# Fetching the selected rows of an attention mask by an indirect DMA instead of a product with a one-hot matrix

## The reference, cut to what matters

```
x = layernorm(x + attention(x))                      # 16 heads of 8, tanh soft cap, causal
weights = x @ router_w + router_b                    # one number a token
sel_idx = sort(top_k(weights, 64)[:63])              # the chosen tokens of a batch
x_sel, pos_sel, w_sel = x[sel_idx], position_ids[sel_idx], weights[sel_idx]
m_sel = attention_mask[b, 0][sel_idx][:, sel_idx]    # 63 x 63 values of a 512 x 512 mask
sc = q @ k.T / sqrt(8) + m_sel                       # rotary attention among the chosen tokens
out = x; out[sel_idx] = processed(x_sel) * w_sel     # plus x for the tokens not above the threshold
x = layernorm(x + out)
```

## Time and profile before

| | us |
|---|---|
| median of 3 runs | 994.78 |
| lowest, highest | 991.25, 1000.37 |
| span of the profiled execution | 992.9 |
| mean granted TensorE clock in it | 0.792 of 2.4 GHz |

### The profile page before, as it was taken

One profiled execution on the slowest core, in us unless ns is written; L12 is line 12 of the kernel. 1 busy time (PEld: TensorE's weight loads), 2 busy tenths in 40 slices (PEclk: granted clock), 3 DMA queues, 4 the chain that ended last, 5 costly groups with the idle time before them and its releaser, 6 DMA issues.

```text
span 992.9 us, 17000 instructions
## 1 busy us (share of the span) xinstructions
PE 777.2 (78%) x5488; PEld 443.0 (45%) x5488; DVE 710.4 (72%) x2141; ACT 610.8 (62%) x403; POOL 412.1 (42%) x776
## 2 busy tenths in 40 slices
PE   3389887989688978898698869898689969764653
PEld 2244343544455444544464445545454445343432
DVE  4632648668868887877887787977887886767444
ACT  0198778668766786677485866677576958800000
POOL 4144425444436444542544443642545344501100
PEclk9997667879788997897697877897697969965555
DMA  5010000002000102000100002000100000000001
GB/s 169 0 33 1 12 12 21 2 2 106 22 1 2 44 1 65 1 1 0 39 25 0 1 0 64 0 1 0 53 0 0 2 20 24 1 1 22 0 1 43
DMA packets 30340, 19.65 MB, mean 20 GB/s; under 512 B 1459, under 2 KB 27587, under 8 KB 30275
## 3 DMA queue, kind: packets, MB, share of 16 engines
q1 hardware_dynamic: 30274, 18.89, 6.3%
HBM read 14.69 MB, written 4.19 MB: 19 GB/s over the span
## 4 chain that ended last, share of the span: by engine, by line
PE 51%; DVE 31%; issue 12%; ACT 3%; POOL 1%; DVEq 1%; POOLq 0%; ACTq 0%
PE ps_s L1123 10%; PE ps_y L1137 9%; PE ps_m L1238 4%; PE ps_a L1187 4%; PE ps_m L1144 3%; DVE junk L893 3%; PE ps_m L1205 3%; PE ps_a L1175 2%; PE ps_a L1168 2%; PE ps_m L1298 2%; PE ps_m L1337 2%; PE ps_m L1284 2%; PE ps_m L1223 2%; ACT pr L664 2%; PE ps_m L1321 1%
## 5 line engine op out<-in xcount | busy, mean ns | idle before, releaser
L652 ACT ACTIVATE th<-ps_s 128x1024 f32<-128x1024 f32 (+1 forms) x256 | 310.1, 1236 | 192.0 <-PE ps_s L1123 186.8
L664 ACT ACTIVATE pr<-th 128x2560 f32<-128x2560 f32 x128 | 298.6, 2334 | 32.8 <-PE ps_y L1137 32.8
L1123 PE MATMUL ps_s<-q_st,k_st 32*128 32x512 f16 (+3 forms) x1024 | 207.9, 338 | 10.1 <-ACT th L652 6.9
L560 POOL TENSOR_SCALAR_AFFINE_SELECT pr<-pr 128x256 f32<-128x256 f32 (+2 forms) x512 | 198.8, 421 | 0.0
L1137 PE MATMUL ps_y<-pr,v_aug 128*32 128x512 f32 (+3 forms) x2048 | 172.1, 482 | 3.4 <-POOL pr L560 3.4
L1123 PEld LDWEIGHTS ps_s<-q_st,k_st 32*128 32x128 f16 x1024 | 83.4, 101 | 101.0 <-issue 55.8
L617 POOL TENSOR_TENSOR pool_mark<-head_of 128x1 f32<-128x1 f32 x128 | 27.3, 213 | 216.0 <-ACT pr L664 215.9
L574 POOL TENSOR_TENSOR st<-qk,st 128x1024 f16<-128x1024 f32 x32 | 73.0, 2301 | 101.7 <-DVE st L800 101.7
L1137 PEld LDWEIGHTS ps_y<-pr,v_aug 128*32 128x32 f32 x2048 | 63.7, 119 | 108.9 <-issue 91.7
L1187 PE MATMUL ps_a<-ident,st 128*128 128x128 f16 x512 | 57.4, 281 | 39.6 <-POOL st L574 23.6
L1187 PEld LDWEIGHTS ps_a<-ident,st 128*128 128x128 f16 x512 | 44.5, 127 | 62.3 <-issue 42.8
(11 more groups left out here) (186 smaller groups left out, 1258.6 us busy)
## 6 DMA issues: line engine op xcount, KB each, us to landing
masks<-in_L_ffn_attention_mask SPq DMA_DIRECT2D x5, 1024.0 KB, 5.9
x_in<-in_L_attn_x SPq DMA_DIRECT2D x16, 256.0 KB, 3.2
x_res<-in_L_attn_x SPq DMA_DIRECT2D x16, 256.0 KB, 3.2
result<-y_out SPq DMA_DIRECT2D x16, 256.0 KB, 2.4
w_sb<-in_L_ffn_w SPq DMA_DIRECT2D x2, 256.0 KB
pr<-in_L_attn_w_q SPq DMA_DIRECT2D x1, 64.0 KB, 1.9
pr<-in_L_attn_w_k SPq DMA_DIRECT2D x1, 64.0 KB, 2.0
pr<-in_L_attn_w_v SPq DMA_DIRECT2D x1, 64.0 KB, 2.0
```

The lines of the kernel that those rows point to most:

```text
L560: return nc.gpsimd.affine_select(out=buf, in_=buf, compare_op=ALU.is_ge, fill=0.0, base=0, pattern=[[0, n], [1, P]] if n > 1 else [[1, P]] ...
L652: nc.scalar.activation(th[:, gi % 2, c0:c1], ps_s[:, c0:c1], ACT.Tanh, scale=1.0 / (QK_SCALE ** 2 * DH ** 0.5 * SOFTCAP))\
L664: nc.scalar.activation(pr[:, gi % 4, :], th[:, gi % 2, :], ACT.Exp, scale=SOFTCAP)\
L1123: last = mm(ps_s[:, c:c + S - P * kb], k_st[32 * j:32 * j + 32, k, g, P * kb:P * kb + P], q_st[32 * j:32 * j + 32, k, g, P * kb:S], start= ...
```

## The change

The chosen rows no longer come by a product. The table `trig` gets a 17th column with the number of the token's row among the 4 x 512 mask rows, so the gathering product brings that number along in `xs`. A new step `sel.row` on POOL, last in the slot of `sel.zb`, waits for `xs`, converts the number to an integer and issues one indirect DMA that reads 128 rows of 2 KB from the mask in HBM into `R`, now a buffer of its own. Step `sel.RT` waits for that DMA. The steps `sel.R` of PE and DVE, the five loads of mask tiles, and the wait of `route.w` for the buffer that `R` shared are gone. POOL's iterations are all written out now instead of looping. In the setup, POOL has one iota, one conversion and a longer first wait more, and DVE and PE wait for 18 instead of 16 setup steps.

```diff
-    [], ["prep.st0/0@1", "sel.R@-1", "prep.st1/0@1"],          # PE_ORDER
+    [], ["prep.st0/0@1", "prep.st1/0@1"],
...
-    ["fin.root1/0@0 & late.root1@-2", "sel.R@-1", "fin.root2/0@0 & late.root2@-2"],     # VE_ORDER
+    ["fin.root1/0@0 & late.root1@-2", "fin.root2/0@0 & late.root2@-2"],
...
-    [], ["prep.sq/0@1", "sel.zb@-1"],                          # POOL_ORDER
+    [], ["prep.sq/0@1", "sel.zb@-1", "sel.row@-1"],
...
-    "sel.R": ["sel.vv1@0"],                                    # BANK_READ
-    "sel.qkT": ["sel.R@0"],
+    "sel.qkT": ["sel.vv1@0"],
...
-        masks = sb("masks", [P, 2, NT, S])
-        trig = sb("trig", [P, NPC, 2 * DH])
+        trig = sb("trig", [P, NPC, 2 * DH + 1])
+        row_i = sb("row_i", [P, NPC], I32)
+        mask_row = sb("mask_row", [P, 1], I32)
...
-        xs = sb("xs", [P, D + 1 + 2 * DH])
+        xs = sb("xs", [P, D + 2 + 2 * DH])
...
-        R = w_wide
+        R = sb("R", [P, S])
...
+            nc.gpsimd.iota(row_i[:, :], pattern=[[P, NPC]], base=0, channel_multiplier=1).then_inc(const_ready, 1)
+            pool.wait_ge(const_ready, 8)
...
+            nc.gpsimd.tensor_copy(trig[:, :, 2 * DH], row_i[:, :]).then_inc(const_ready, 1)
+            pool.wait_ge(const_ready, 15)
...
+            def sel_row(q, _):
+
+                ve["sel"].wait(pool, q, "xs")
+                if q > 0:
+                    pool.wait_ge(mask_fetched, q * 16)
+                pl["sel"].done(nc.gpsimd.tensor_copy(mask_row[:, :], xs[:, D + 1 + 2 * DH:]), "row", q)
+                pl["sel"].wait(pool, q, "row")
+                pe["sel"].wait(pool, q - 1, "RT")
+                nc.gpsimd.indirect_dma_start(
+                    R[:, :], None, amask.rearrange("m o s j -> (m o s) j"),
+                    bass.IndirectOffsetOnAxis(ap=mask_row[:, 0:1], axis=0), bounds_check=MASKS * S - 1,
+                    oob_is_err=False).then_inc(mask_fetched, 16)
...
-            iterations(pool, body, 3, PAIRS - 2)
+            for p in range(-1, PAIRS + 3):
+                body(p)
...
-                if k == 0:
-                    pe["sel"].wait(v, b.pair - 1, "RT")
...
-                ve["sel"].wait(t_, q, "R")
+                t_.wait_ge(mask_fetched, q * 16 + 16)
                 bank_free("sel.RT", q)
```

More of the change, by code:

```diff
@@ L67 @@
     "sel": ["xs", "ss"] + newton("r1", 1) + newton("r1", 2) +
-        ["hn", "ET", "hnT", "cosp", "sin0", "sin1", "rope", "vv0", "vv1", "R", "qkT", "RT", "msel"],
+        ["hn", "ET", "hnT", "cosp", "sin0", "sin1", "rope", "vv0", "vv1", "qkT", "RT", "msel"],
     "att": ["sc0", "mx0", "sub0", "sc1", "mx1", "sub1", "den", "rden", "PT0", "PT1", "o0", "o1", "oT", "x1f",
@@ L77 @@
     "route": ["wrow"],
-    "sel": ["gather", "ET", "hnT", "qkv", "R", "qkT", "RT", "msel"],
+    "sel": ["gather", "ET", "hnT", "qkv", "qkT", "RT", "msel"],
     "att": ["S0", "S1", "P0T", "P1T", "PV", "oT", "wo", "h2T", "w1"],
@@ L84 @@
     "route": ["xw"],
-    "sel": ["zb0", "zb1"],
+    "sel": ["zb0", "zb1", "row"],
     "att": ["kw0", "kw1", "hh", "hu"],
@@ L400, in build @@
         zeroed = sem("zeroed")
-        mask_loaded = sem("mask_loaded")
+        mask_fetched = sem("mask_fetched")
         x_in_loaded = [sem(f"x_in_loaded{i}") for i in range(2)]
@@ L461, in _ @@
         def _(sp):
-            def load_mask(m, k):
-                sp.dma_start(masks[:, k], amask[m, 0].rearrange("(c p) j -> p c j", p=P)).then_inc(mask_loaded, 16)
             for i, (w, t) in enumerate(((w_q, 0), (w_k, 1), (w_v, 2), (w_o, 3))):
@@ L478, in _ @@
             sp.dma_start(pos_i[:, :], pos.rearrange("b (c p) -> (b c) p", p=P)).then_inc(weights_in, 16)
-            for k in range(2):
-                load_mask(k, k)
             def load_res(b, k):
@@ L505, in body @@
                     load_x(Batch(p, 4), 0)
[L507 to L511, removed]
                 if live(p - 2, PAIRS):
@@ L528, in _ @@
             nc.gpsimd.iota(slot_i[:, :], pattern=[[1, SLOTS]], base=0, channel_multiplier=0).then_inc(const_ready, 1)
-            pool.wait_ge(const_ready, 7)
+            nc.gpsimd.iota(row_i[:, :], pattern=[[P, NPC]], base=0, channel_multiplier=1).then_inc(const_ready, 1)
+            pool.wait_ge(const_ready, 8)
             nc.gpsimd.affine_select(out=ident[:, :], in_=ident[:, :], compare_op=ALU.not_equal, fill=1.0, base=0,
@@ L540, in _ @@
             nc.gpsimd.tensor_copy(slot_no[:, :], slot_i[:, :]).then_inc(const_ready, 1)
-            pool.wait_ge(const_ready, 13)
+            nc.gpsimd.tensor_copy(trig[:, :, 2 * DH], row_i[:, :]).then_inc(const_ready, 1)
+            pool.wait_ge(const_ready, 15)
             nc.gpsimd.affine_select(out=head_of[:, :], in_=head_of[:, :], compare_op=ALU.is_ge, fill=0.0, base=DH - 1,
@@ L605, in att_hu @@
                 pl["att"].done(mul(hu[:, :], hq[:, :], hb[:, :]), "hu", q)
-            table = {"prep.sq": prep_sq, "prep.lo": prep_lo, "route.xw": route_xw, "sel.zb": sel_zb, "att.kw": att_kw,
+            table = {"prep.sq": prep_sq, "prep.lo": prep_lo, "route.xw": route_xw, "sel.zb": sel_zb, "sel.row": sel_row, "att.kw": att_kw,
                      "att.hh": att_hh, "att.hu": att_hu}
@@ L680, in _ @@
             v.wait_ge(attn_weights_in, 16 * 4)
-            v.wait_ge(const_ready, 16)
+            v.wait_ge(const_ready, 18)
             for half in range(2):
@@ L929, in sel_gather @@
                 ve["late"].wait(v, q - 1, "proc")
-                ve["sel"].done(nc.vector.tensor_copy(xs[:, :], ps_m[:, 0:D + 1 + 2 * DH]), "xs", q)
+                ve["sel"].done(nc.vector.tensor_copy(xs[:, :], ps_m[:, 0:D + 2 + 2 * DH]), "xs", q)
             sel_ET = copy_step("sel", "ET", lambda: nc.vector.tensor_copy(ET[:, :], ps_m[:, :]),
                                [(pe["late"], lambda q: q - 1, "sc1")])
-            sel_R = copy_step("sel", "R", lambda: nc.vector.tensor_copy(R[:, :], ps_m[:, :]),
-                              [(ve["route"], lambda q: Batch(q, 1), f"eq{NT - 1}")])
             def sel_squares(q, _):
@@ L1077, in _ @@
                      "route.row": route_row, "route.ge": route_ge, "route.eq": route_eq, "route.rank": route_rank,
-                     "sel.xs": sel_gather, "sel.ET": sel_ET, "sel.R": sel_R, "sel.ss": sel_squares, "sel.hn": sel_hn,
+                     "sel.xs": sel_gather, "sel.ET": sel_ET, "sel.ss": sel_squares, "sel.hn": sel_hn,
                      "sel.RT": sel_RT, "sel.hnT": sel_hnT, "sel.qkv": sel_qkv, "sel.msel": sel_msel,
@@ L1098, in _ @@
             tr = nc.tensor.transpose
-            t_.wait_ge(const_ready, 16)
+            t_.wait_ge(const_ready, 18)
             t_.wait_ge(attn_weights_in, 16 * 4)
@@ L1224, in sel_gather @@
                     for c in range(NT):
-                        last = mm(ps_m[rows, D + 1:D + 1 + 2 * DH], E[:, c, rows],
+                        last = mm(ps_m[rows, D + 1:D + 2 + 2 * DH], E[:, c, rows],
                                   trig[:, NT * trig_row(Batch(q, k)) + c, :], start=(c == 0), stop=(c == NT - 1))
@@ L1345, in _ @@
                      "fin.yT": fin_yT, "fin.wo": fin_wo, "route.wrow": route_wrow, "sel.gather": sel_gather,
-                     "sel.ET": sel_ET, "sel.R": sel_R, "sel.RT": sel_RT, "sel.hnT": sel_hnT, "sel.qkv": sel_qkv,
+                     "sel.ET": sel_ET, "sel.RT": sel_RT, "sel.hnT": sel_hnT, "sel.qkv": sel_qkv,
                      "sel.msel": sel_msel, "sel.qkT": sel_qkT, "att.S0": lambda q, _: att_scores(q, 0),
```

## The result

The changed kernel takes **1026.3 us** (median of four runs, 1024.4 to 1026.9) against 996.6 before (991.3 to 1000.4, four runs on the same chip): ratio 1.028, 95% interval 1.024 to 1.033. It is 2.8% slower where 993 was forecast, and lies outside the range. The profiled execution has a span of 1025.2 us, 32.3 more than before.

A forecast was written before the change was run, and what follows sets the result against it. PE and DVE hand work to each other, neither alone setting the pace. Gain 11.2 us (6.3 in pairs 0 to 5, 4.9 in 6 and 7) against 11.1 of cost: no change, forecast 993 us, range 981 to 1009.

The forecast's parts named there:

- the wait at `pv.0`: Second batch's `pv.0` on PE waits for POOL's masking, 2.4 us late; 1.0 us passes on in pair 4, 9.1 in all.
- the clock there: The wait at `pv.0` may let the clock fall one step earlier; 1.5 us in all.
- the price of a `pv` block at the lower clock: A `pv` step takes 3.91 us at 1.2 GHz and 2.36 at 2.4, a factor of 1.65; used behind the removed product.
- 24.4 minus 13.2: Removing the product gains 24.4 us through PE; the low clock behind its place takes back 13.2 in six pairs.
- The reading of the cover: Three of the product block's 5.6 us in pair 4 are hidden behind DVE; the next step starts 2.6 us earlier.
- the upper bound of that term, 22: Clock cost in six pairs if the whole stretch behind the removed product runs at 1.2 GHz; 13.2 was taken.
- The last pair: No other work fills the product's block there, so DVE's path gives 3.8 us of gain.
- pair 6: No transposes stand behind the product's block there, so DVE is the later one; 1.1 us of gain.
- The DMA: The fetched rows land before `sel.RT`, in pair 4 25 us behind the issue, so nothing of the transfer shows.
- The loads, the 17th column and the written-out loop: Removing five mask loads, widening the gather product and copy, and writing out POOL's loop: 0 each.
- the three things that I said would show me wrong: Issue under 0.6 or over 2 us on POOL, clock 1.00 behind the transposes, or PE waiting for the DMA.
- The long issue on POOL: Rival, chance 0.18: the DMA issue behind `xs` is long, 7 us per us; 1009 us at 3.5 us of issue.

The follow-up runs named there:

- e1: The changed kernel with `sel.row` moved six slots later on POOL, behind the two masking groups `pv.0` waits for; 994.0 us, ratio to before 0.997.
- e2: The kernel before with `sel.row` added into a spare buffer, product kept, POOL's loop written out, one set of mask tiles; 1029.0 us, ratio 1.029.
- e6: The changed kernel with eight unused products added on PE ahead of `pv.0`, where PE waits; 1010.5 us, ratio to before 1.014.
- e5: The changed kernel without the indirect DMA, POOL's wait and conversion kept, mask left out of the result; 1008.4 us, ratio to before 1.008.
- e10: The changed kernel with `sel.row` six slots later on POOL and three unused products where the mask product stood; 986.3 us, ratio to before 0.987.
- e4: The kernel before with POOL's loop written out and nothing else; 994.8 us, ratio 0.999.
- e3: The changed kernel without `sel.row`, `R` a constant zero and the mask left out; 991.3 us, ratio to before 0.994.

## Why the prediction was wrong

**The step that failed: the wait at `pv.0`**, the term that priced the issue on POOL with "two groups ... 2.4 us late, and `pv.0` of PE with them" and "1.0 us passes on", 9.1 us in all, and the clock there at "1.5 us in all". The mechanism is the one named (e1, e2); the size is 31 us instead of 10.6. Two things were mis-sized. POOL was later than worked out: 3.5 us, since between the conversion and the DMA that reads its result POOL stands idle 0.79 us, which I had not counted, and the masking groups took 0.36 more behind it (3.60 us for 3.24). The wait for `xs`, 1.11 against 0.95, the conversion, 0.30 against 0.25, and the issue, 1.06 against 1.2, were right. With 1.4 of slack 2.1 us pass on instead of 1.0, and in the whole kernel 16 us. The larger error is the clock: I put it at 1.5 us in all, and it takes 15 us (e6), 1.3 to 2.1 us at each `pv.0`. A right size of the wait would not have saved the sum: in e5 waits of 1.24 to 1.56 us brought the low clock too, in six of seven pairs. The prediction used the price of a `pv` block at the lower clock only at the other end of the pair, and misread the row: 3.91 us is a block in which the clock rose. A window over it, and a `pv` block of the same trace that is at 1.2 GHz throughout:

```profile
603.58:607.49 3.91, 3.91 (x34) 1.31 (x34) 2.89 (x6) 0.00 (x0) 1.04 (x1) 0.59 0.91 259
...
120.60 4.50 PE L1137 MATMUL ps_y<-pr,v_aug 128*32 128x512 f32 x32
```

So the factor is 4.50 / 2.36 = 1.91 and not 1.65.

**The product was worth even less than 24.4 minus 13.2.** The reading of the cover was right: without the product the step behind it starts 0.06 us after DVE's copy, PE idles 2.3 us ahead of it, the clock stands at 0.50, as forecast, and in e1 it comes 2.5 us sooner behind `xs` (19.9 us against 22.4), where 2.6 was worked out. Over six pairs it starts 17.0 us sooner (19.2 by the rows; the prediction's 19.5 is a slip of 0.3). But the clock took all of it, not half: `pv.1` needs 4.29 to 4.50 us, not 3 to 3.9, which is 12.3 us in six pairs, the transposes ahead of it take 5 us more, and the second column of the table is 52.9 us in e1, 52.8 before. These 17 us lie nearer the upper bound of that term, 22, than its 13.2, which rested on the assumption that the clock would rise as long after the start of the block as it had after that of the product; in e1 it hardly rose within `pv.1` in any of the six pairs. e10 shows the other side: with the clock up the same removal is worth 12.7 us at this place.

**The last pair** gave 3.5 us in e1, for 3.8, and **pair 6** nothing, for 1.1. **The DMA** landed 3.4 us after its issue and no instruction of PE waited for it, as said. **The loads, the 17th column and the written-out loop** show no cost (e4 for the last; e3, which has all three changes, is faster than the kernel before). Of the three things that I said would show me wrong none came: the issue takes 1.06 us, the clock behind the transposes is low, nothing waits for the DMA. They watched the terms I was unsure of, and the failure came from one that I had thought small.

**The rivals.** The long issue on POOL had the right place and direction and the wrong price: at 1.06 us it was not long, and its rule, 7 us for each us of lateness, held only until the clock fell with it. (By that rule and 993 the kernel is level with the one before at an issue of 1.5 us and 1% slower at 2.9, not at 1.9 and 2.6.) The Trainium skill (page "SBUF — State Buffer", section "SBUF: two separate sides") has such a DMA wait for its descriptors while VectorE holds the shared port; the issue here took 1.06 us in the changed kernel and 1.63 at the late place (medians), beside a busy VectorE both times, so the 1.9 us more of issue in the estimate of about 1006 were not there. The rows landed 3.4 and 4.0 us after the issue; no run has this DMA beside an idle VectorE, so whether any of that was such a wait is not shown.

Of a clock that falls in every round the Trainium skill tells too (page "TensorE: Matmul & The Clock Gate", section "HAM oscillation — how this bites in real kernels"): a kernel whose TensorE waits in each tile pays the low clock in each tile anew. This case agrees, with 15 us in seven pairs for waits of 3.2 to 3.8 us.

**What stays open.** Why one of four waits of 1.56 us left the clock up in e5, no run settles, nor why the issue takes 0.6 us longer at the late place. Nor is it shown why the stretch from `RT` to the next `xs` is 3 to 6 us longer than before in the three other kernels of the table.

## What to carry to other kernels

Where a step is added on an engine that is not the bottleneck, look at what stands behind it in that engine's order and who waits for it at that moment; the same step behind three masking groups cost nothing here, and some 30 us in front of them. Price a new gap of TensorE twice: the time that passes the slack, and the next block at 1.2 GHz by a row of that same block at that clock. Work that fills a gap may be holding the clock up, and to remove it can gain nothing until something else, even an unused product, stands there.

## What was not expected of the hardware

- POOL stood idle some 0.8 us between its own conversion and the indirect DMA that reads the converted numbers, in each of eight pairs (6.5 us in all) and in every kernel that had the step.
- The issue of the indirect DMA of 128 rows took POOL 1.06 us at the first place and 1.63 at the later one. It landed in 3.4 and 4.0 us.
- Added products made a kernel faster: eight in front of `pv.0` brought the ratio from 1.028 to 1.014, three in the gap of e1 from 0.997 to 0.987.
- Within one execution (e5) a wait of 1.56 us was followed by a block at the lower clock for all or most of its length, 3.74 to 4.50 us, and in another pair by one at 2.4 GHz, 2.36 us.
